# Transposing a tile once: the FFN input made in place from the transposed mix input

## The reference

```python
xn = layernorm(x, eps=1e-5)
# branch 1: recurrent attention on xn mixed with the token before
xm = xn * time_mix + shift(xn) * (1 - time_mix)
k = exp(minimum(xm @ Wk.T, 60)); v = xm @ Wv.T; r = xm @ Wr.T
wkv, sum_k = decayed sums over earlier tokens of k * v and of k, per head
attn = (sigmoid(r) * wkv / sum_k) @ Wo.T
# branch 2: FFN with ternary weights on xn, normalised a second time
z = (xn - mean(xn)) * rsqrt(var(xn) + 1e-3) * gamma + beta
g = max(abs(z))                       # over the whole input
y = (clip(z * 128 / g) @ ternary(W)) * (g * mean(abs(W)) / 128)
out = x + attn + y
```

## Time and profile before

| | us |
|---|---|
| median of three runs (lowest, highest) | 891.59 (891.33, 891.74) |
| time of the profiled execution | 891.49 |
| its span, first to last instruction | 889.7 |
| TensorE busy | 867.1 (97%) |
| VectorE busy | 764.8 (86%) |
| ScalarE busy | 510.3 (57%) |
| GpSimd busy | 215.2 (24%) |

### The profile page before, as it was taken

The page is one execution under the profiler, slowest core; times in us unless marked ns, Lnnn a source line. Parts: engine busy times, 40 slices in busy tenths (PEclk is TensorE's granted clock), DMA queues, the critical chain, the costliest instruction groups (busy, mean ns, idle before and its releaser), DMA issues.

```text
span 889.7 us, 12792 instructions
## 1 busy us (share of the span) xinstructions
PE 867.1 (97%) x3984; PEld 714.5 (80%) x3984; DVE 764.8 (86%) x1278; ACT 510.3 (57%) x834; POOL 215.2 (24%) x242
## 2 busy tenths in 40 slices
PE   3989999999999999999999999999999999999998
PEld 2778888888888888888888888888888888888886
DVE  5998999989897999989897897878978888789684
ACT  5584767667594757566564554545546536365441
POOL 5552326242452425240030100200201103011000
PEclk9999999999999999999999999999999999999999
DMA  8222415041423224045643245324451443424311
GB/s 283 108 83 88 149 54 184 13 171 54 165 71 135 101 82 154 12 172 136 212 145 115 84 154 189 125 75 141 153 175 57 157 141 96 154 93 142 95 48 47
DMA packets 59841, 107.13 MB, mean 120 GB/s; under 512 B 7712, under 2 KB 7712, under 8 KB 59808
## 3 DMA queue, kind: packets, MB, share of 16 engines
q1 hardware_dynamic: 59808, 106.73, 35.1%
HBM read 64.76 MB, written 41.96 MB: 120 GB/s over the span
## 4 chain that ended last, share of the span: by engine, by line
PE 90%; DVE 3%; issue 2%; POOL 2%; ACT 1%; DMA 0%; SPq 0%; POOLq 0%; DVEq 0%; ACTq 0%
PE kvr L513 18%; PE kvr L515 18%; PE kvr L514 18%; PE out_banks L552 7%; PE out_banks L554 7%; PE out_banks L534 6%; PE out_banks L533 6%; PE out_banks L531 6%; PE transposed L466 2%; PE out_banks L466 2%; DVE bn_stats L842 1%; POOL normed L1174 1%; POOL own_stats L1156 1%; POOL own_stats L1157 1%; DMA x<-in_x 0%
## 5 line engine op out<-in xcount | busy, mean ns | idle before, releaser
L1247 POOL TENSOR_TENSOR evacuated<-normed,mix_over_ffn_row 128x512 f32<-128x512 f32 x28 | 49.0, 1751 | 339.0 <-DVE ffn_lo L922 339.0
L513 PE MATMUL kvr<-xm_hi,wk_hi 128*128 128x512 f32 x256 | 103.7, 405 | 2.6 <-DVE xm_lo L922 2.6
L513 PE MATMUL kvr<-xm_hi,wv_hi 128*128 128x512 f32 x256 | 102.9, 402 | 2.2 <-DVE wv_lo L927 1.3
L513 PE MATMUL kvr<-xm_hi,wr_hi 128*128 128x512 f32 x256 | 102.7, 401 | 0.0
L515 PE MATMUL kvr<-xm_hi,wk_lo 128*128 128x512 f32 x256 | 101.0, 395 | 0.0
L514 PE MATMUL kvr<-xm_lo,wk_hi 128*128 128x512 f32 x256 | 100.7, 394 | 0.0
L515 PE MATMUL kvr<-xm_hi,wv_lo 128*128 128x512 f32 x256 | 100.2, 391 | 0.0
L515 PE MATMUL kvr<-xm_hi,wr_lo 128*128 128x512 f32 x256 | 100.1, 391 | 0.0
L531 PE MATMUL out_banks<-wo_hi,rwkv_hi 128*128 128x512 f32 x256 | 100.0, 390 | 0.0
L534 PE MATMUL out_banks<-wo_hi,rwkv_lo 128*128 128x512 f32 x256 | 99.7, 389 | 0.0
L514 PE MATMUL kvr<-xm_lo,wr_hi 128*128 128x512 f32 x256 | 99.7, 389 | 0.0
(11 more groups left out here) (140 smaller groups left out, 1922.7 us busy)
## 6 DMA issues: line engine op xcount, KB each, us to landing
other<-ffn_input SPq DMA_DIRECT2D x64, 256.0 KB, 5.1
x<-in_x SPq DMA_DIRECT2D x15, 1024.0 KB, 5.8
other<-in_x SPq DMA_DIRECT2D x8, 1024.0 KB, 5.8
ffn_input<-evacuated SPq DMA_DIRECT2D x32, 256.0 KB, 4.4
ffn_input<-parked SPq DMA_DIRECT2D x32, 256.0 KB, 2.2
attn_scratch<-x SPq DMA_DIRECT2D x8, 1024.0 KB, 4.2
parked<-attn_scratch SPq DMA_DIRECT2D x8, 1024.0 KB, 6.7
out<-parked SPq DMA_DIRECT2D x8, 1024.0 KB, 5.2
```

The lines of the kernel that those rows point to most:

```text
L513: nc.tensor.matmul(KVR[:, m, :], hi, XH[t][:, ch, :], start=(ch == 0), stop=False)
L1247: G.tensor_tensor(U[:, n % RING, :], XN[:, ch, :], BC[:, :], ALU.mult).then_inc(pool_v, 1)
```

## The change

The own FFN slots no longer transpose. TensorE skips them (`is_virtual`), and the counts of its slots are taken without them (`pe_slots_before`). When ScalarE evacuates a mix slot it first copies the transposed chunk, unscaled, into a new buffer Y, which lies where phase B keeps its FFN parts. VectorE's `own_ffn_input` multiplies that chunk in place by a row RROW that holds, for each token, the second scale over the first; ScalarE's evacuation of an own FFN slot then reads Y in place of a bank. For the tile of batch 0 that the opening transposes, four copies into Y are added in the opening, whose transposes go to other banks.

The ratio comes from GpSimd's `ffn_scale`, now four steps and not six, and is written to memory by SyncE in the form of the existing row store and loaded back, repeated over the partitions. The second normalising of each own tile, on GpSimd and on ScalarE, is gone. VectorE makes the products of the second own tile at the ends of groups 10 (slot 12), 11 (slot 13) and 12 (slots 14 and 15), those of the next batch's first tile after the batch's last `add_out`, and those of batch 0's first tile before its first group.

The core of the diff:

```diff
+        Y = nc.alloc_sbuf_tensor_at("own_normed", [P, CH, TILE], F32, offset=FFN_ROOM)
+        RROW = nc.alloc_sbuf_tensor_at("ffn_over_mix_rows", [P, 2, TILE], F32, offset=FFN_ROOM + 4 * CH * TILE)
...
+            sp.wait_ge(pool_ratio, 1)
+            sp.dma_start(ratio_row[0, 0].rearrange("(q p) -> p q", p=P), ratio[:, 0, :],
+                         allow_slow_non_contiguous=True).then_inc(s_ratio[0], 16)
             sp.wait_ge(dve_w, 2 * CH)
             sp.dma_start(X[1][:, :, :], x_t[0, 1]).then_inc(s_x[1], 16)
+            sp.wait_ge(s_ratio[0], 32)
+            sp.dma_start(RROW[:, 0, :], ratio_row[0, 0].rearrange("(o n) -> o n", o=1)
+                         .to_broadcast([P, TILE])).then_inc(s_rrow[0], 16)
...
+            def store_ratio(b, t):
+
+                sp.wait_ge(pool_ratio, 2 * b + t + 1)
+                sp.dma_start(ratio_row[b, t].rearrange("(q p) -> p q", p=P), ratio[:, t, :],
+                             allow_slow_non_contiguous=True).then_inc(s_ratio[t], 16)
+
+            def load_ratio(b, t, reader_done):
+
+                sp.wait_ge(s_ratio[t], 16 * b + 32)
+                sp.wait_ge(dve_z, reader_done)
+                sp.dma_start(RROW[:, t, :], ratio_row[b, t].rearrange("(o n) -> o n", o=1)
+                             .to_broadcast([P, TILE])).then_inc(s_rrow[t], 16)
...
                 store_ffn_input(b, 7)
                 store_row(b, 0)
+                store_ratio(b, 1)
+                load_ratio(b, 1, virtual_before(b, CH))
                 store_ffn_input(b, 12)
...
-                for n in range(14, 19):
+                for n in range(14, 18):
                     store_ffn_input(b, n)
                 if not is_last:
-                    sp.wait_ge(pe_t, slots_before(b, "A", first_slot("ffn_other1") + CH))
+                    store_ratio(b + 1, 0)
+                store_ffn_input(b, 18)
+                if not is_last:
+                    sp.wait_ge(pe_t, pe_slots_before(b, "A", first_slot("ffn_other1") + CH))
                     sp.dma_start(ZA[:, :, :], x_t[b + HALF + 1, 0]).then_inc(s_oth, 16)
                 store_ffn_input(b, 19)
                 store_row(b, 1)
+                if not is_last:
+                    load_ratio(b + 1, 0, virtual_before(b, len(SLOTS)))
...
-                    if ph == "B":
+                    if ph == "B" or n is not None and is_virtual(n):
                         n = None
...
+                virtual = ph == "A" and is_virtual(n)
+                if virtual:
+                    act.wait_ge(dve_z, virtual_before(b, n) + 1)
...
                     if ph != "P":
+                        if copy_own:
+                            nc.scalar.activation(Y[:, ch, :], bank, ACT.Copy)
                         nc.scalar.activation(U[:, r, :], bank, ACT.Copy, scale=tmx[:, ch:ch + 1])
...
+            def own_ffn_input(b, n):
+
+                kind, ch = SLOTS[n]
+                t = int(kind[-1])
+                dve.wait_ge(s_rrow[t], 16 * b + 16)
+
+                if t:
+                    dve.wait_ge(act_u, slots_before(b, "A", first_slot("mix_own1") + ch) + 1)
+                else:
+                    dve.wait_ge(act_first, 1)
+                    dve.wait_ge(act_u, slots_before(b, "A", first_slot("mix_next0") + ch - len(SLOTS)) + 1)
+                V.tensor_tensor(Y[:, ch, :], Y[:, ch, :], RROW[:, t, :], ALU.mult).then_inc(dve_z, 1)
...
+            OWN_FFN_AT = {10: [12], 11: [13], 12: [14, 15]}
...
+                    if ph == "A":
+                        for n in OWN_FFN_AT.get(g, ()):
+                            own_ffn_input(b, n)
...
                 if ph == "A" and not last_a:
+                    for ch in range(CH):
+                        own_ffn_input(b + 1, ch)
                     tile_stats(b + 1, ph, "other0", is_last)
...
-                step(i, "A", 7, G.tensor_tensor(st[:, 4, :], st[:, 3, :], half_neg[:, :], ALU.pow))
-                step(i, "A", 8, G.tensor_tensor(dst[:, 2, :], st[:, 4, :], dst[:, 0, :], ALU.mult))
-                step(i, "A", STEPS, G.tensor_tensor(dst[:, 3, :], st[:, 5, :], dst[:, 2, :], ALU.mult))
+                pool.wait_ge(s_ratio[t], 16 * b + 16)
+                pool.sem_inc(pool_past, 1)
+                step(i, "A", STEPS, G.tensor_tensor(ratio[:, t, :], st[:, 3, :], half_neg[:, :], ALU.pow))
+                pool.sem_inc(pool_ratio, 1)
...
-                ffn_scale(*call(b, "own1"), own[:, 1])
-                pool.wait_ge(pe_t, slots_before(b, "A", first_slot("mix_own1") + CH))
-                normalise(XN, X[1], own[:, 1], 1, pool_xn)
+                ffn_scale(*call(b, "own1"), own[:, 1], b, 1)
                 other(b, "other1")
```

More of the change, by code:

```diff
@@ L131, in mixed_decay_kernel @@
         inv = sb("mix_over_ffn_stat", [P, 2, Q])
+        ratio = sb("ffn_over_mix_stat", [P, 2, Q])
         gamb = sb("gamma_beta", [P, CH])
@@ L154, in mixed_decay_kernel @@
         s_bc = sem("row_loaded")
+        s_ratio = [sem(f"ratio_row_stored{t}") for t in range(2)]
+        s_rrow = [sem(f"ratio_row_loaded{t}") for t in range(2)]
         s_mix = sem("mix_input_loaded")
@@ L203, in mixed_decay_kernel @@
         pool_v = sem("pool_mix_input")
+        pool_ratio = sem("pool_ratio_row")
+        dve_z = sem("dve_own_ffn_input")
         dve_past = sem("dve_past_wait")
@@ L221, in slots_before, with is_virtual, pe_slots_before, virtual_before @@
             return n if ph == "P" else CH + len(SLOTS) * b + n
+        def is_virtual(n):
+            return SLOTS[n][0].startswith("ffn_own")
+        def pe_slots_before(b, ph, n):
+            if ph == "P":
+                return n
+            per_batch = sum(not is_virtual(k) for k in range(len(SLOTS)))
+            return CH + per_batch * b + sum(not is_virtual(k) for k in range(n))
+        def virtual_before(b, n):
+            return 2 * CH * b + sum(is_virtual(k) for k in range(n))
         def ffn_stores_before(b, n):
@@ L251, in normed_count @@
             if ph == "A":
-                return 4 * b + [k for k in SLOT_KINDS if "other" not in k].index(kind) + 1
-            return 4 * HALF + 2 * (b - HALF) + ["mix_own1", "mix_next0"].index(kind) + 1
+                return 2 * b + ["mix_own1", "mix_next0"].index(kind) + 1
+            return 2 * HALF
         def stats_number(b, ph, tile):
@@ L288, in shifted @@
             return E[:, n % 2, :] if ph == "P" and n > 1 else WS[:, n % 2, :]
-        first_banks = [TB[:, :]] + [KVR[:, i, :] for i in range(3)]
+        first_banks = [OUT[:, q, :] for q in range(Q)]
         def slot_bank(ph, n):
@@ L672, in normalise @@
                 ffn = kind.startswith("ffn")
-                i = 4 * b if kind == "ffn_own0" else stats_number(b, ph, tile)
-                act.wait_ge(pool_step, STEPS + steps_before(i, ph) + (OTHER_STEPS if "other" in kind else STEPS if ffn else MIX_STEPS))
+                i = stats_number(b, ph, tile)
+                act.wait_ge(pool_step, STEPS + steps_before(i, ph) + (OTHER_STEPS if "other" in kind else MIX_STEPS))
                 for q in ACT_CHUNKS:
@@ L707, in _ @@
                 high_part(0, "P", m)
-            act.wait_ge(pool_step, STEPS + STEPS)
-            for q in ACT_CHUNKS:
-                last = nc.scalar.activation(XN[:, q, :], X[0][:, q, :], ACT.Identity,
-                                            bias=own[:, 0, 3, q:q + 1], scale=own[:, 0, 2, q:q + 1])
-            last.then_inc(act_xn, 1)
             weight_hi("r")
+            for ch in range(CH):
+                last = nc.scalar.activation(Y[:, ch, :], first_banks[ch], ACT.Copy)
+            last.then_inc(act_first, 1)
             act.wait_ge(dve_w, 3 * CH)
@@ L757, in batch @@
                     part1_first = ahead_of_part2(n)
+                    keep = not (last_a and n is not None and SLOTS[n][0] == "mix_next0")
                     if part1_first:
-                        evacuate(b, ph, n)
+                        evacuate(b, ph, n, keep)
                     hurry = ph == "A" and g == GROUPS - 1
@@ L1123, in _ @@
             weight_lo("o")
+            for ch in range(CH):
+                own_ffn_input(0, ch)
             with dve.Fori(0, HALF - 1) as b:
@@ L1181, in _ @@
             normalise(XN, X[0], own[:, 0], 0, pool_xn)
-            ffn_scale(0, 0, own[:, 0])
-            pool.wait_ge(pe_t, CH)
-            normalise(XN, X[0], own[:, 0], 1, pool_xn)
+            ffn_scale(0, 0, own[:, 0], 0, 0)
             pool.wait_ge(s_w[1], 16)
```

52 lines of the change are left out of this document (25 added, 27 removed).

## The result

The changed kernel takes 916.58 us in the median of four runs (914.03 to 918.52), the kernel before 891.66 beside it: a ratio of 1.027, 95% interval 1.024 to 1.031. The forecast was 915.5. The profiled execution is the slowest of the four, 918.52 for a span of 916.7, 27.0 us more than the profiled one of before; the medians differ by 24.9.

What follows compares the result with a forecast made beforehand. VectorE was taken as the tighter loop after the change (95.8 us a batch, TensorE 95.1). 24.8 - 0.6 + 2.5 - 2.7 = +24.0 on 891.5 gave 915.5 us, own range 900 to 927, 8 in 10 from 893 to 938.

Steps and rivals of the forecast that it cites:

- Removed: TensorE, phase A: eight own FFN transposes fewer a batch, 3.8 us, 15.4 in all, if TensorE stays the bound.
- Products: VectorE: eight added 128x512 products a batch at 0.62 us, 5.0 a batch, giving 95.8 us of work.
- The new wait: VectorE at group 10 waits 5.6 us for the loaded ratio row, delaying group 12's low parts: +6.2 a batch, +24.8.
- The rest of the loop: Low parts to next M: seven products added (4.3 us), VectorE's waits for TensorE removed (4.5): -0.2, three times, -0.6.
- Start and end: Four products on VectorE before batch 0: +2.5 us; from the last low parts TensorE runs to phase B sooner: -2.7.
- The row in time: Store plus load under 9 us, so no VectorE wait at group 10: 893, or 876 if TensorE binds; chance 0.16.
- Stacked stores: The new row's store proceeds only after the old one lands, row 9.2 us later: 952, half of that 934; chance 0.22.
- TensorE restarting slowly: Slow matmuls after new gaps at slot 8 and group 12: 2.9 us a group, four times 11.5, 927; no separate chance.

Runs made afterwards that it cites:

- Neither: The changed kernel, but the loop's eight products a batch work on one column and wait for no row; 893.13 us, ratio 1.001 to the kernel before.

## Why the prediction was right

The direction was right for the reason given: a new wait for the row, and more work on VectorE, outweigh the transposes. That the sum (915.5 for 916.58) and the batch (104.9 for 104.8) agree so closely is luck, as the terms show.

**Removed.** "3.8 a batch, if TensorE stays the bound" was never seen whole: with products, wait and reload gone the shortest batch is 96.2, 2.7 under the kernel before, and 95.1 was forecast for TensorE. The condition did not hold. "Neither" keeps 0.9 of the 3.8 us, in part (1.4 to 1.9) since the reload of own tile 0 binds next; the rest was not found. The text looked for the next bound among the engines and not in that chain of transfers.

**Products.** 0.62 us each was right, 5.0 a batch; their price with no wait is 2.5 us a batch over "neither". VectorE is then busy for 94.1 to 94.8 of 100.0 to 101.0 us, so it did not become the loop without gaps that the sum follows (95.8 of work).

**The new wait.** Place, mechanism and number (four, and a fifth one of 2.2 us at the end of batch 1 for the row of the next own tile 0, which the text held to be in time) were right. The size was off: +4.6 a batch instead of +6.2. The store lets go after 8.0 to 11.0 us and not 11.1, the load takes 3.1 to 5.0 and not 3.5, and VectorE comes 0.9 later in batch 2. The wait by itself costs 13.9 of the 25 us.

**The rest of the loop.** -0.6 was wrong; it was +4.6. Two of its steps failed. The four products at the batch's end stand ahead of the other tile's statistics, so TensorE waits 1.9 to 3.9 us at slot 4; the version with the statistics first has no such wait and is 5.2 us faster. And the text took VectorE's waits for TensorE's work off whole and set no new ones in their place. The named ones, 4.5 us, did go for the most part, but new ones came: for the reload (1.0 and 1.4 us, in batches 0 and 2), for the row of the next own tile 0 (2.2, in batch 1), and in each batch 0.5 for ScalarE at the gate. From the low parts to the next M VectorE's idle time fell by 2.3 us a batch, while its busy time rose by 3.8 (forecast 4.3).

**Start and end.** +4.1 for +2.5: the four products come as costed. The wait on the product ahead of slot 0's evacuation was to cost nothing "where the product is early", and in the opening it is not early: TensorE stands 4.1 us, and the slower clock behind the gap was put at nothing too. At the end +0.1 for -2.7; no experiment was made on it, but in "neither", without product and wait, that part is only 0.4 shorter than before.

**Rivals.** The row in time: no; from the store's issue to VectorE's start 12.4 to 14.1 us pass, and it would have held under 9.0. Stacked stores: no; alone on its way the store takes 8.0 to 9.2. TensorE restarting slowly: in part. Windows of 5 us behind the opening's gap of 4.1 us and behind batch 0's of 3.8 at group 12 show 0.50 and 0.66, and a batch 0.95 to 0.98; this is the second of the two:

```profile
75.00:80.00 5.00, 5.00 (x17) 3.75 (x16) 4.96 (x9) 2.07 (x4) 0.00 (x0) 0.66 0.16 56
```

The matmuls of 0.63 us, which the text saw beside a granted clock of 1.00, are those of the 0.50 window here; they start 0.43 us apart and not 0.23, so one costs 0.20 more, not 0.24. The gap's length alone does not decide: behind group 12's gap of 3.2 us in batch 1 some 14 matmuls ran so, behind the one of 3.15 in batch 2 none. From the first M to the end of phase A the rows have some 40 of them, by estimate 8 us of TensorE's time; how much of it reached the result was not separated.

## What to carry to other kernels

When work is taken off the tightest engine, list what would bind next, and list chains of transfers (store, reload, statistics) beside the engines: here three quarters of the gain did not show, and such a chain held up to half of it. A value that goes to memory and back as a row took 12 to 14 us here, whether 512 or 128 values were stored; look at what stands behind its first reader on an in-order engine, and put that reader last. Moving work from VectorE to GpSimd gave nothing here, since both then ran at once: time the neighbours too.

## What the runs showed of the hardware

A store of 4-byte values from 128 partitions takes 8 to 12 us in the medians of the lists (ratio row 8.1, a quarter of it 8.7, the other row 9.8 in the change, 11.1 before, 12.0 with the ratio's store first), where 256 KB in whole lines take 2.1. Why the two rows differ was not tried. The Trainium skill (DMA: Bandwidth & Descriptors, Anatomy of one DMA) gives a fixed cost of about 2 us, most of it the write receipt, for transfers that GpSimd issues; these come from SyncE. The runs agree that the number of values does not matter here, and disagree with the 2 us by a factor of four.

GpSimd's products of 128x512 went with VectorE instructions that were 0.9 to 1.1 us longer each, the short copy too (0.17 to 1.08). Its normalising did not: in batch 2 of the change it ran from 264.0 to 266.9, and VectorE's instructions at 263.72 and 264.92 took their usual 1.28 and 0.69 us. The Trainium skill (SBUF — State Buffer, SBUF: two separate sides) says that the two engines share a pair of ports, which an instruction that needs it holds to its end; the rows of the products fit this, but the ports themselves are in no row.
